# Turned layer inputs from DRAM, normalised on VectorE, and the residual in three pieces, in a fused attention and mixture-of-experts kernel

## The reference

```python
# B = 16 batches of T = 256 rows of D = 256; H = 8 heads of 128; E = 8 experts, top 2, F = 1024
x = x + tanh(g_xattn) * attn(ctx_1024, layernorm(x))
x = x + tanh(g_ffn)   * moe(layernorm(x))

def attn(x, latents, ...):                 # x is ctx_1024 ("media"), latents = layernorm(x)
    xn = layernorm(x, gamma_media, beta_media)
    ln = layernorm(latents, gamma_lat, beta_lat)
    q  = ln @ Wq + bq
    k, v = split(concatenate([xn, ln], axis=1) @ Wkv + bkv)      # 512 keys
    return softmax(q k^T / sqrt(128)) v @ Wo + bo                # per head

def moe(x, ...):
    gates = (x @ Wg + bg) / (1 + 1e-6);  weights, i = top_k(gates, 2)
    return sum over the 2 experts of softmax(weights) * (silu(x @ W1[e] + b1[e]) @ W2[e] + b2[e])
```

## Time and profile before

| | |
|---|---|
| median of 3 runs | 1544.16 us (1540.41 to 1545.47) |
| the profiled execution, its own time | 1537.72 us |
| its span, first to last instruction | 1536.0 us |
| TensorE busy | 1499.6 us, 98% |
| VectorE, ScalarE, GpSimd busy | 1112.4, 950.0, 601.7 us |
| attention stage (128 steps) | up to about 1080 us |

### The profile page before, as it was taken

How to read it: one execution, slowest core, us unless ns; L and a number is a source line. 1 busy time by engine, 2 the same in 40 slices (tenths; PEclk the granted TensorE clock), 3 DMA queues, 4 the chain that set the end, 5 groups by cost and what they waited for, 6 DMA issues and landing times. The chain is left out here.

```text
span 1536.0 us, 29968 instructions
## 1 busy us (share of the span) xinstructions
PE 1499.6 (98%) x10446; PEld 1381.2 (90%) x10446; DVE 1112.4 (72%) x2689; ACT 950.0 (62%) x2057; POOL 601.7 (39%) x714
## 2 busy tenths in 40 slices
PE   8999999999999999999999999999889999999997
PEld 6889898898988888898888989888889999999996
DVE  7677777777777777777777777687796666666685
ACT  5555656556565555555565555655787777777775
POOL 5323424333342433434233342233455444444443
PEclk9999999999999999999999999999999999999999
DMA  4000100000000010000000000012855555445563
GB/s 158 10 22 8 22 8 22 28 1 29 8 22 8 22 29 8 22 8 22 8 22 28 8 22 8 8 27 85 227 126 132 129 147 141 129 126 151 136 173 83
DMA packets 57823, 91.13 MB, mean 59 GB/s; under 512 B 8617, under 2 KB 44774, under 8 KB 57550
## 3 DMA queue, kind: packets, MB, share of 16 engines
q1 hardware_dynamic: 41710, 70.19, 14.2%
q0 software_dynamic: 15824, 18.98, 7.0%
q10 hardware_dynamic: 144, 0.05, 0.0%
HBM read 70.91 MB, written 18.29 MB: 58 GB/s over the span
## 5 line engine op out<-in xcount | busy, mean ns | idle before, releaser
L885 POOL TENSOR_SCALAR probs<-probs,rsum 128x512 f32<-128x512 f32 x256 | 174.1, 692 | 532.4 <-DVE rsum L1559 532.2
L1091 ACT ACTIVATE pt_hi<-turn 128x512 fp32r<-128x512 f32 x256 | 139.1, 595 | 238.2 <-PE turn L1239 236.8
L910 POOL DMA_INDIRECT out_rows<-yo,token x71 | 121.6, 1713 | 206.7 <-DMA out_rows<-yo,token 134.5
L1676 DVE TENSOR_TENSOR ht_lo<-hs,ht_hi 128x512 fp32r<-128x512 f32 x142 | 98.2, 691 | 118.1 <-ACT ht_hi L1058 113.3
L1553 DVE TENSOR_REDUCE smax<-score 128x1 f32<-128x512 f32 x256 | 169.6, 684 | 13.1 <-PE score L189 12.7
L992 ACT ACTIVATE probs<-score,nbias 128x512 f32<-128x512 f32 x256 | 173.0, 685 | 3.9 <-DVE nbias L1555 3.8
L1049 ACT ACTIVATE hs<-ph,vecs 128x256 f32<-128x256 f32 (+1 forms) x284 | 114.1, 457 | 93.5 <-PE ph L189 82.4
L1786 DVE TENSOR_TENSOR pt_lo<-turn,pt_hi 128x512 fp32r<-128x512 f32 x256 | 164.1, 682 | 8.3 <-ACT pt_hi L1091 8.1
L187 PE MATMUL py<-w_hi,ht_lo 128*128 (+1 forms) x568 | 162.7, 286 | 3.2 <-DVE ht_lo L1676 3.2
L189 PE MATMUL py<-w_hi,ht_hi 128*128 (+1 forms) x568 | 160.6, 283 | 0.0
L188 PE MATMUL py<-w_lo,ht_hi 128*128 (+1 forms) x568 | 160.5, 283 | 0.0
(11 more groups left out here) (245 smaller groups left out, 4703.2 us busy)
## 6 DMA issues: line engine op xcount, KB each, us to landing
w_raw<-in_L_ffn_W SPq DMA_DIRECT2D x45, 1024.0 KB, 15.6
xhat_rows<-rows SPq DMA_DIRECT2D x16, 264.0 KB, 2.2
x_raw<-in_x SPq DMA_DIRECT2D x16, 256.0 KB, 3.2
c_raw<-in_ctx SPq DMA_DIRECT2D x16, 256.0 KB, 3.3
out_rows<-x SPq DMA_DIRECT2D x16, 256.0 KB, 2.5
xg<-xhat_rows,token POOLq DMA_INDIRECT x71, 4.5
out_rows<-yo,token POOLq DMA_INDIRECT x71
v_raw<-in_L_xattn_Wkv SPq DMA_DIRECT2D x2, 512.0 KB, 8.0
```

The lines of the kernel that those rows point to most:

```text
L885: last = pool.tensor_scalar(probs[n % 2][:, t, :], probs[n % 2][:, t, :], rsum[:, n % 2, t:t + 1], 1.0, ALU.mult, ALU.mult)
L910: pool.indirect_dma_start(out=A["out"], out_offset=bass.IndirectOffsetOnAxis(ap=token[:, u:u + 1].bitcast(U32), axis=0), in_=yo_of(t)[:, s ...
L1091: act.activation(pt[0][:, 2 * t:2 * t + 2, :], turn[t][:, :].rearrange("p (j i) -> p j i", j=2), ACT.Copy).then_inc(s_pthi, 1)
```

## The change

The host passes two more arrays, `x` and `ctx_1024` already turned. SP loads them (`load_turned`) into `zin`, which takes the place of `z`. GpSimd's `prepare` now makes only the negated mean and the factor of each row (`norms`); SP writes these 4 x 256 values of 4 bytes to DRAM and reads them back spread over all partitions (`spread_norms`, 512 KB). VectorE adds the one (`centre`) and multiplies by the other (`normalise_turned`), each in two instructions of 128x512 for a batch, and ScalarE applies gamma and beta from SBUF (`scale_turned`). The `z` units and their ring positions are gone. `residual` is split into `add_bias` (tail of h=1), `residual` (h=2, between the readings of the `k` and the `q` unit) and `row_moments` (h=3, the same place). `norm_rows` on GpSimd moves from h=1 to h=3; the unit `t` stays at h=3. `prepare_a` and `prepare` move one step later. `load_w1(0)` stands behind the wait for `s_kvt`.

```diff
-A_STEP = 3
+A_STEP = 4
+N_STEP = 6
@@ plan_units
-        if h == Z_STEP and b + 1 < B:
-            units += [("z", (b + 1, k)) for k in range(KD)]
@@ sync
+            def load_turned(c):
+                if c == 1:
+                    sp.wait_ge(s_full, KD)
+                else:
+                    sp.wait_ge(s_zt, c - 1)
+                for name, cols in (("x_turned", slice(T, KEYS)), ("ctx_turned", slice(0, T))):
+                    sp.dma_start(zin[:, :, cols], A[name][c].rearrange("(k p) t -> p k t", p=P)).then_inc(s_turned_in, 16)
+
+            def spread_norms(c):
+                sp.wait_ge(s_rsa, c)
+                sp.wait_ge(s_z, c + 1)
+                for tiles, cols in ((slice(0, TT), slice(T, KEYS)), (slice(TT, JT), slice(0, T))):
...
+                        for r in range(2):
+                            sp.dma_start(dram["spread"][c, r, cols].rearrange("(j p) -> p j", p=P), norms[:, r, tiles])\
+                                .then_inc(s_norms_out, 16)
+                sp.wait_ge(s_norms_out, 64 * c)
+                if c == 1:
+                    weights_split(sp, "k1")
+                else:
+                    sp.wait_ge(s_zin, KD * (c - 1))
+                sp.dma_start(spread[:, :, :].rearrange("p r t -> p (r t)"),
+                             dram["spread"][c].rearrange("r t -> (r t)").partition_broadcast(P)).then_inc(s_spread, 16)
...
                 if b + 3 < B:
                     load(b + 3)
+                    load_turned(b + 3)
+                    spread_norms(b + 3)
                 sp.wait_ge(s_rows, b + 1)
@@ gpsimd, prepare
-                pow_rstd("a", rs_a, 4, s_rsa)
-                negate(mv_a)
-                own.wait()
-                pool.wait_ge(s_rsa, c)
-                pool.wait_ge(s_full, number["z", (c - 1, KD - 1)] + 1)
-                for t in range(TT):
-                    norm(z[:, TT + t, :], x_raw[c % 3][:, t, :], mv_a, rs_a, t)
-                for t in range(TT):
-                    last = norm(z[:, t, :], c_raw[c % 2][:, t, :], mv_a, rs_a, TT + t)
-                last.then_inc(s_z, 1)
+                if c >= 2:
+                    pool.wait_ge(s_norms_out, 64 * (c - 1))
+                own.wait()
+                pool.tensor_tensor(norms[:, 1, :], ve["a"][:, 0:JT], minus_half[:, 0:JT], ALU.pow).then_inc(s_rsa, 1)
+                pool.tensor_scalar(norms[:, 0, :], mv_a[:, :, 0], -1.0, 0.0, ALU.mult, ALU.add).then_inc(s_z, 1)
@@ gpsimd, the loop over the steps, behind normalise(i)
+                if i == 4:
+                    split_kv(1)
+                if h == T_STEP and 1 <= b < B:
+                    norm_rows(b - 1)
                 if h == A_STEP and b + 2 < B:
                     prepare(b + 2)
-                if h == Z_STEP and b + 1 < B:
+                if h == Z_STEP and 1 <= b < B - 1:
                     split_kv(b + 1)
-                if h == R_STEP and 1 <= b < B:
-                    norm_rows(b - 1)
@@ scalar
+                if i == 3:
+                    scale_turned(1)
+                if i % H == 1 and 1 <= i // H < B - 1:
+                    scale_turned(i // H + 1)
@@ vector
+            def centre(c, k):
+                dve.wait_ge(s_turned_in, 32 * c)
+                dve.wait_ge(s_spread, 16 * c)
+                own.mark(dve.tensor_tensor(zin[:, k, :], zin[:, k, :], spread[:, 0, :], ALU.add))
+
+            def normalise_turned(c, k):
+                own.wait()
+                dve.tensor_tensor(zin[:, k, :], zin[:, k, :], spread[:, 1, :], ALU.mult).then_inc(s_zin, 1)
...
                 for u in steps[i]:
                     if u[0] in "kq":
                         read_unit(*u)
+
+                    if u[0] == "k":
+                        if h == R_STEP + 1 and 1 <= b < B:
+                            residual(b - 1)
+                        if h == R_STEP + 2 and 1 <= b < B:
+                            row_moments(b - 1)
+                        if h == A_STEP and b + 2 < B:
+                            prepare_a(b + 2, 1)
+                        if i in (2, 3):
+                            centre(1, i - 2)
+                        if h == N_STEP and b + 2 < B:
+                            centre(b + 2, 0)
+                        if h == N_STEP + 1 and b + 2 < B:
+                            normalise_turned(b + 2, 0)
+                        if h == 0 and 1 <= b < B - 1:
+                            centre(b + 1, 1)
+                        if h == 1 and 1 <= b < B - 1:
+                            normalise_turned(b + 1, 1)
                 if i < STEPS:
                     reciprocal_sum(i)
+                if i in (2, 3):
+                    normalise_turned(1, i - 2)
```

More of the change, by code:

```diff
@@ L282, in build @@
             lists=nc.dram_tensor("expert_lists", (LISTS, P), F32, kind="Internal").ap(),
+            spread=nc.dram_tensor("mean_and_factor", (B, 2, KEYS), F32, kind="Internal").ap(),
         )
@@ L286, in build @@
             zt = alloc(first, "zt", [P, KD, KEYS])
-            z = alloc(first, "z", [P, JT, D])
+            with ExitStack() as rows_of_first:
+                z = alloc(rows_of_first, "z", [P, JT, D])
+            zin = alloc(first, "z_turned", [P, KD, KEYS])
             kvt0 = [alloc(first, f"kvt0_{s}", [P, KD, KEYS], F32R) for s in pair]
@@ L427, in layer @@
         pad_ids = sb("pad_ids", [P, P])
-        raw.update(k1=sb("k1_raw", [P, KD, INNER - FIRST_W]), q1=sb("q1_raw", [P, KD, INNER - FIRST_W]),
-                   o0=sb("o0_raw", [P, H // 2, D]), o1=sb("o1_raw", [P, H // 2, D]))
+        norms = sb("norms", [P, 2, JT])
+        with ExitStack() as raws:
+            raw.update(k1=alloc(raws, "k1_raw", [P, KD, INNER - FIRST_W]),
+                       q1=alloc(raws, "q1_raw", [P, KD, INNER - FIRST_W]),
+                       o0=alloc(raws, "o0_raw", [P, H // 2, D]), o1=alloc(raws, "o1_raw", [P, H // 2, D]))
+        spread = sb("spread", [P, 2, KEYS])
         x2, rows = [x2_0, x2_1], [rows0, rows1]
@@ L697, in load_weights @@
                         sp.dma_start(r[:, :, :], src).then_inc(s_win[name], 16)
+            def load_turned(c):
[9 more added lines that the diff above has]
+                for tiles, cols in ((slice(0, TT), slice(T, KEYS)), (slice(TT, JT), slice(0, T))):
+                    with nc.allow_non_contiguous_dma(reason="a value of each row"):
+                        for r in range(2):
[8 more added lines that the diff above has]
+                             dram["spread"][c].rearrange("r t -> (r t)").partition_broadcast(P)).then_inc(s_spread, 16)
             load(0)
@@ L715, in _ @@
             load(2)
+            load_turned(2)
+            spread_norms(2)
             def load_w2(at):
@@ L999, in read_unit, with scale_turned @@
                 act.wait_ge(s_full, n + 1)
-                if kind == "z":
-                    c, k = at
-                    if c:
-                        act.wait_ge(s_kvt, c)
+                act.activation(x2t[:, :, :], src[:, :].rearrange("p (k t) -> p k t", k=KD), ACT.Copy).then_inc(s_aread, 1)
+            def scale_turned(c):
+                act.wait_ge(s_zin, KD * c)
+                act.wait_ge(s_kvt, c)
+                for k in range(KD):
                     for s in range(2):
-                        last = act.activation(zt[:, k, s * T:(s + 1) * T], src[:, s * T:(s + 1) * T], ACT.Identity,
+                        cols = slice(s * T, (s + 1) * T)
+                        last = act.activation(zt[:, k, cols], zin[:, k, cols], ACT.Identity,
                                               scale=gamma[:, s, k:k + 1], bias=beta[:, s, k:k + 1])
-                else:
-                    last = act.activation(x2t[:, :, :], src[:, :].rearrange("p (k t) -> p k t", k=KD), ACT.Copy)
-                last.then_inc(s_aread, 1)
+                last.then_inc(s_zt, 1)
             def hi_x(t):
@@ L1193, in unit @@
                                        [s[:, j, :] for s in pt], j == 0, j == JT - 1)
-                elif kind == "z":
-                    c, k = at
-                    pe.wait_ge(s_z, c + 1)
-                    for j in range(JT):
-                        last = pe.transpose(dst[:, j * P:(j + 1) * P], z[:, j, k * P:(k + 1) * P], ident[:, :])
                 elif kind == "t":
@@ L1533, in weigh, with add_bias @@
                 last.then_inc(s_rows, 1)
-            def residual(b):
+            def add_bias(b):
                 dve.wait_ge(s_proj, b + 1)
@@ L1540, in residual @@
                     .then_inc(s_projr, 1)
+            def residual(b):
                 dve.wait_ge(s_projr, b + 1)
@@ L1545, in residual, with row_moments @@
                                          in1=x_raw[b % 3][:, :, :], op0=ALU.mult, op1=ALU.add).then_inc(s_x2, 1)
+            def row_moments(b):
                 dve.wait_ge(s_x2, b + 1)
@@ L1807, in _ @@
                     constants()
-                if h in (A_STEP - 1, A_STEP) and b + 2 < B:
-                    prepare_a(b + 2, h - A_STEP + 1)
```

(9 more changed lines are left out.)

16 lines of the change are left out of this document (10 added, 6 removed).

## The result

The changed kernel takes 1633.5 us in the median of three runs (1629.5 to 1637.5), beside 1542.3 us (1539.9 to 1545.5, 4 runs) for the kernel before in the same session: ratio 1.059, 95% interval 1.055 to 1.063. A fourth run took 3410.7 us, which nothing on record explains, and is left out (with it the median is 1635.5). The kernel is slower, as forecast, but by 91 us and not by 37: the time lies outside the range (1562 to 1596). The profiled execution took 1629.51 us with a span of 1627.8; before it was 1536.0, so 91.8 us have to be found.

A forecast was written before the change was run, and what follows sets the result against it. TensorE, 98% busy, was taken as the bound. Against 1537.7 us: batches 14 x 1.75 = +24.5, last batch +3.1, start -2.35, clock +12, together +37, so 1575; on the median 1581, range 1562 to 1596.

The forecast's parts named there:

- the stall at the unit `t`: End of h=3: TensorE idle 3.2 us for `rows`, with `normalise` ahead of `norm_rows` on GpSimd; +1.75 us a batch.
- h=2 at 7.90, no wait at `kt_lo`: At h=2 the 8 transposes of `z` and 0.30 us of waiting leave: 9.25 - 7.90 = 1.35 us.
- The start without its late wait: Step 2 loses 8 transposes (1.05 us), step 3 its 1.30 us wait for `kt_lo`: together -2.35 us.
- VectorE's new work in the gaps: `centre` and `normalise_turned`, 0.75 us an operation, stand in four gaps of 0.95 us: nothing on the path.
- Hidden, by 3.6 us: Spreading through DRAM: stores 2.1 us, read back 5.1, landing at 17.5 from the start of h=4; `centre` due at 21.1.
- the row of `early_names`: Profile row of a transfer of 4-byte elements, 2.1 us, taken for the four stores of 256 values.
- the spread values are late: Rival: stores and read back over 10.8 us, `centre` holds VectorE; 3 us late costs about 28 us, 1609; chance 0.05.
- the clock: Behind the 15 stalls of TensorE at h=3, half followed by a low stretch: 8 x 1.5 = 12 us.
- the 2.8 us of idle time: Trace before, between 1079.5 and 1086: TensorE idle 2.8 us in one piece while the clock stayed at 1.00.
- the stall's step: Step h=3 with TensorE's wait for `rows`: 11.46 us long where it was 8.36.

The follow-up runs named there:

- the move alone: Kernel before with only `norm_rows` on GpSimd moved from h=1 to h=3, behind `normalise`: 1604.6 us.
- the packed kernel: Changed kernel, spread values stored by one DMA of 32 bytes for each of 128 partitions, VectorE reading with a stride of 32 bytes: 1579.9 us.
- the fast kernel: Changed kernel with one store of 32-byte pieces, `row_moments` in the tail of h=2, `norm_rows` ahead of `normalise` at h=3: 1522.3 us, ratio 0.989.
- one store: Changed kernel with one DMA instead of four writing the 1024 values of 4 bytes to the same places: 1627.9 us.

## Why the prediction was wrong

**Right.** The direction and its cause: the stall at the unit `t`, 3.09 us for 3.2 foretold, from `normalise` ahead of `norm_rows`; the move alone costs 62 us. h=2 at 7.90, no wait at `kt_lo`. The start without its late wait: 67.4 us of steps 0 to 7 in the packed kernel, -2.3 for -2.35. VectorE's new work in the gaps costs nothing as such: even with 1.15 us instead of 0.69 for `centre` and `normalise_turned` the fast kernel's TensorE never waits for them.

**The step that failed** is "Hidden, by 3.6 us", the spreading through DRAM. Its term for the stores was 2.1 us, from the row of `early_names`; they took 9.5. That row is 4-byte elements too, but 768 of them, read from DRAM; these are 1024 written to it. From the end of `prepare` to the landing I had 7.2 us, it took 14.4, and 10.8 were allowed. The rival "the spread values are late" had it right, mechanism and place, with its threshold, and at 0.05 it had far too little chance: the bound from the nearest row was taken as the value although direction and count both differed. It cost 14 x 1.46 = 20.4 us in h=6 and h=7, and 14.8 at the start (+12.4 where -2.35 was foretold), together 35 of the 55 us that the forecast missed. With the store packed and all else as changed the kernel took 1579.9 us, beside a forecast of 1581; that it came so near is in part luck, since the clock fell 6 times there and not 8, and h=3 and the expert stage were longer than foretold. The rival's own price was off too: 3.6 us late gave 14 x 2.6 = 36 us by its rule, while in the gap VectorE passes on to TensorE only 1.2 of its 2.8 us of waiting. And the start wasn't in its price at all: there GpSimd has `split_kv(1)` ahead of `prepare(2)`, the stores are issued 13.8 us behind the start of h=4 where 10.3 was reckoned, and take 10.3 us.

**A term mis-sized: the clock.** I took half of the stalls, by the 2.8 us of idle time that did no harm at the change of stage. 13 of 15 were followed by a low stretch, at 1.7 us or a little less each; about 20 us where 12 were taken, of which 14 x 1.16 = 16 lie in h=4 and the rest in the ends of h=3 and in the last batch. And I counted it behind the unit `t` alone: it also fell behind TensorE's waits of 3.7 and 6.1 us at the start, which cost 1.7 us in step 3 and 2.9 in step 7 (9.85 and 10.75 long, 8.11 and 7.90 in the packed kernel); these stand in the 14.8 above. How often it falls is not fixed: in four kernels with the same stall it was 6 (packed), 11 (the move alone), 13 (the changed one) and 14 times in 15 (one store), so half was inside what happens, at its lower end. The case of the earlier trace rows was one draw and not a limit. The same 2.77 us at the change of stage is there in all twelve kernels, and in eight of them the clock fell behind it. In the changed kernel the 32 us around it stand at 0.95, before they were at 1.00:

```profile
1081.10:1113.10 32.00, 29.56 (x247) 1.00 0.88 230
```
```profile
1163.50:1195.50 32.00, 28.86 (x227) 0.95 0.88 231
```

That is 1.6 us, of the expert stage's 9.3. The Trainium skill, "TensorE: Matmul & The Clock Gate", Part 1, "What's actually happening", has idle time lead back to the half clock. I had let the single row of 2.8 us speak against it; over 60 places with 2.9 to 3.3 us the traces agree with it 44 times, and 12 times in 15 with 2.2 to 2.4 us.

**A term mis-sized: the stall's step.** h=3 was to be 11.46 and is 11.64 where the clock doesn't fall, 11.80 on the mean: 14 x 0.34 = 4.8 us over.

**Not foreseen: the expert stage**, +9.3 us. 4.9 of it are the waits for gathered rows at 1241.46 (2.35, 0.56 before) and 1582.61 (3.06, none before), with 2.5 by the clock (6.3 us lost in the stage, 3.8 before); the rest, some 2 us, wasn't assigned. Part of the waits goes with the 4-byte stores, as told above.

The sum by the measured terms: 35 (spread) + 9 (expert stage) + 5 (h=3) + 6 (clock outside h=3, last batch included) is 55, what the forecast was short of.

## What to carry to other kernels

When a producer is moved later on an engine that takes its stream in order, write out what stands ahead of it there, and put it ahead of all that isn't needed sooner; here two lines put above `normalise`, with the moments a step earlier, took 68 us from the changed kernel's 1629.5. A transfer that is to be hidden has to be priced by a row of the same direction and the same size and count of pieces; without such a row the rival "late" gets a real chance, and its cheapest cure (values of a partition side by side) is tried in the same edit. And a wait of TensorE in the middle of dense work is to be counted with a stretch at half clock behind it: here it followed most waits of 2.2 us and more, some of 1.4 to 2.2 us and none of those under 1.4.

## What the runs showed of the hardware

- **Small stores.** 1024 values of 4 bytes into DRAM: 8.4 to 10.9 us by one DMA, 9.0 to 11.2 by four; the same 4 KB as 128 pieces of 32 bytes: 1.4 us. A broadcast that was issued ahead of them on the same queue took 6.0 us in the median of 15 (3.3 to 11.1) and 3.7 without them (3.4 to 4.2).
- **The clock.** At the unit `t` it fell behind 44 of 60 idle pieces of 2.9 to 3.3 us (6 to 14 of 15 in four kernels) and 12 of 15 of 2.2 to 2.4 us, behind none of 15 of 0.9 to 1.2 us and none of 15 of 0.5 to 0.7 us. At h=6 of the seven kernels with a late spread (91 places) it fell behind both of 3.0 and 3.3 us, 7 of 23 of 1.4 to 2.2 us and none of 66 under 1.4 us. At the change of stage, 2.77 us, it fell in 8 of 12 kernels. Most falls cost 1.7 us of TensorE's time.
- **VectorE with a stride.** An operation on 128x512 fp32 values took 0.68 to 0.69 us with all operands in a row and 1.15 to 1.17 us where one was read at steps of 32 bytes. The Trainium skill, "SBUF — State Buffer", Specifications (TRN2), says that SBUF is read in lines of 16 bytes and that each access which crosses to a new one pays; the traces agree, with some 0.47 us more for 512 values.
